# Pre-norm transformer block on one core: normalised tokens split in place and turned by DMA transposes

## The reference

```python
x = x + attn(layernorm(x), W_qk, W_v, slope)
x = x + ffn(layernorm(x), w_gate, w_up, w_down)

def attn(x, W_qk, W_v, slope):          # causal, one head of 128
    scores = (x @ W_qk) @ x.T / sqrt(128) + (kpos - qpos) * slope
    return softmax(where(qpos >= kpos, scores, -inf)) @ (x @ W_v.T)

def ffn(x, w_gate, w_up, w_down):       # int32 weights times 1/127, hidden width 384
    return (silu(x @ w_gate.T) * (x @ w_up.T)) @ w_down.T
```

## Time and profile before

| what | us |
|---|---|
| median of 3 runs (144.57 to 145.28) | 144.62 |
| the profiled execution, its own time | 145.67 |
| its span, first to last instruction | 143.9 |
| PE, DVE, ACT, POOL busy in the span | 122.8, 120.7, 110.7, 97.6 |

### The profile page before, as it was taken

How to read it: one execution, slowest core, us unless ns; L and a number is a source line. 1 busy time by engine, 2 the same in 40 slices (tenths; PEclk the granted TensorE clock), 3 DMA queues, 4 the chain that set the end, 5 groups by cost and what they waited for, 6 DMA issues and landing times.

```text
span 143.9 us, 3450 instructions
## 1 busy us (share of the span) xinstructions
PE 122.8 (85%) x1215; PEld 91.9 (64%) x1215; DVE 120.7 (84%) x341; ACT 110.7 (77%) x251; POOL 97.6 (68%) x157
## 2 busy tenths in 40 slices
PE   0239658999999999999999998979998899999942
PEld 0028345867987769978779776657755656675541
DVE  0729989998697996969996969999879999988781
ACT  4034588999976999949999769985699978999830
POOL 6490769964993454992438943798999999646810
PEclk9999999999999999999999999999999999999995
DMA  4997000000000000000000000000000222022204
GB/s 129 221 244 190 0 0 2 7 2 0 5 0 0 5 0 2 5 0 0 0 5 0 5 0 2 2 5 0 5 0 0 77 77 66 12 73 77 77 0 146
DMA packets 9811, 5.18 MB, mean 36 GB/s; under 512 B 448, under 2 KB 9792, under 8 KB 9792
## 3 DMA queue, kind: packets, MB, share of 16 engines
q1 hardware_dynamic: 9792, 4.92, 12.2%
HBM read 2.82 MB, written 2.10 MB: 34 GB/s over the span
## 4 chain that ended last, share of the span: by engine, by line
PE 50%; DVE 23%; ACT 9%; POOL 7%; DMA 4%; issue 3%; SPq 2%; DVEq 0%
PE work_ps L556 7%; POOL hidden_lo L411 6%; PE attn_ps L571 5%; PE attn_ps L573 4%; PE attn_ps L572 4%; PE score_ps L504 4%; PE score_ps L506 4%; DVE probsT_lo L824 4%; PE score_ps L505 4%; DMA wd_int<-in_L_ffn_w_down_dram 4%; DVE biased L841 3%; PE score_ps L595 2%; PE score_ps L592 2%; DVE stats L726 2%; ACT silu L1069 2%
## 5 line engine op out<-in xcount | busy, mean ns | idle before, releaser
L571 PE MATMUL attn_ps<-v_hi,probsT_hi 128*128 128x128 f16 x144 | 25.8, 219 | 3.0 <-DVE xs L851 2.4
L824 DVE TENSOR_TENSOR probsT_lo<-work_ps,probsT_hi 128x512 f16<-128x512 f32 (+3 forms) x48 | 25.2, 552 | 3.5 <-ACT probsT_hi L1007 3.4
L1007 ACT CAST probsT_hi<-work_ps 128x512 f16<-128x512 f32 (+3 forms) x48 | 21.4, 484 | 7.7 <-PE work_ps L556 7.4
L992 ACT ACTIVATE probs<-biased,neg_max 128x128 f32<-128x128 f32 (+7 forms) x32 | 25.0, 783 | 1.9 <-DVE neg_max L841 1.9
L841 DVE CUSTOM_DVE_ANT_0 biased<-score_ps,bias,neg_score_scale 128x128 f32<-128x128 f32 (+7 forms) x32 | 25.8, 806 | 0.6 <-PE score_ps L506 0.6
L573 PE MATMUL attn_ps<-v_hi,probsT_lo 128*128 128x128 f16 x144 | 25.8, 219 | 0.0
L572 PE MATMUL attn_ps<-v_lo,probsT_hi 128*128 128x128 f16 x144 | 25.8, 219 | 0.0
L556 PE MATMUL work_ps<-ident,probs 128*128 128x128 f32 x144 | 21.4, 274 | 0.2 <-DVE probsT_lo L824 0.2
L411 POOL TENSOR_TENSOR hidden_lo<-hidden,hidden_hi 128x512 f16<-128x512 f32 x13 | 17.6, 1375 | 5.1 <-ACT hidden_hi L1075 5.1
L556 PEld LDWEIGHTS work_ps<-ident,probs 128*128 128x128 f32 x144 | 16.5, 141 | 3.2 <-DVE probsT_lo L824 0.5
L437 POOL TENSOR_TENSOR xT_lo<-whole,xT_hi 128x512 f16<-128x512 f32 x8 | 9.3, 1163 | 13.6 <-ACT whole L986 13.6
(11 more groups left out here) (135 smaller groups left out, 346.7 us busy)
## 6 DMA issues: line engine op xcount, KB each, us to landing
out_dram<-xs SPq DMA_DIRECT2D x7, 256.0 KB, 2.7
xs<-in_L_attn_x_dram SPq DMA_DIRECT2D x3, 512.0 KB, 7.4
xs<-in_L_attn_x_dram SPq DMA_DIRECT2D x2, 256.0 KB, 3.0
out_dram<-xs SPq DMA_DIRECT2D x2, 128.0 KB, 1.9
wgu_int<-in_L_ffn_w_gate_dram SPq DMA_DIRECT2D x1, 192.0 KB, 3.1
wgu_int<-in_L_ffn_w_up_dram SPq DMA_DIRECT2D x1, 192.0 KB, 3.4
wd_int<-in_L_ffn_w_down_dram SPq DMA_DIRECT2D x1, 192.0 KB, 5.1
wqk_in<-in_L_attn_W_qk_dram SPq DMA_DIRECT2D x1, 64.0 KB, 2.9
```

Source lines behind the costliest of these rows:

```text
L571: pe.matmul(attn_ps[:, 0:D], p_hi, v_j, start=(j == 0), stop=False)
L824: dve.tensor_tensor(probsT_lo[:, i % 2, cols], work_ps[:, bank, 0:n], probsT_hi[:, i % 2, cols], ALU.subtract).then_inc(work_emptied, 1)
L992: act.activation(probs[:, i % 2, 0:n], biased[:, i % 2, 0:n], ACT.Exp, bias=neg_max[:, i:i + 1], scale=-1.0, accum_out=prob_sum[:, i:i + 1 ...
L1007: act.copy(probsT_hi[:, i % 2, CW * h:CW * h + n], work_ps[:, bank, 0:n]).then_inc(probsT_hi_ready, 1)
```

## The change

Normalisations 0 and 1 stay as they were. For 2 and 3 (LN1 of batches 2 and 3) and 4 to 7 (all LN2), PE transposes nothing: ACT casts `xn` in `SBUF` to `xn_hi` (`token_high`), POOL subtracts into `xn_lo` (`token_low`), and SP issues one DMA transpose for each part and half (`turn`; 24 in all, 128 KB each, ahead of all stores in SP's queue). `x2T_hi` and `x2T_lo` get room for all eight chunks. The copies of x to `whole` and the lo parts from it go, for q they stay. DVE's `split_x2` goes. `down` alternates between two PSUM banks.

Statistics move: DVE takes those of 2 in round 0, steps 0 to 3; those of b+3 in rounds 0 to 2, steps 4 to 7; of 6 in the last round, steps 0 to 3; of 7 as before. So LN2 of batches 0 and 1 is normalised in rounds 2 and 3, and each POOL job of a round has its place by a written order. `token_high` stands in ACT's stream at the places of `tokens_at`: normalisation 2 in round 0, step 7, and round 1, step 0; normalisation b+2 in round b, steps 5 and 6 (b = 1, 2, 3); 6 behind the silus of chunks 0 and 1; 7 behind those of chunks 3 and 4.

Core of the diff (the rest replaces run-time indices, no longer needed, and renames the counts of the banks):

```diff
+    BY_DMA = 2
+    NROUND = 2 * B
+    def parts_at(b, i):
+        if b == B - 1 or i == 0:
+            return []
+        return [part for part in prologue[i - 1:i] if part[0] != "xT" or b + 1 < BY_DMA]
...
-        x2T_hi, x2T_lo = (part[:, B % 2, :].rearrange("p (c n) -> p c n", c=2) for part in (xT_hi, xT_lo))
+        x2T_hi = sb("x2T_hi", [P, NCH, CW], F16)
+        x2T_lo = sb("x2T_lo", [P, NCH, CW], F16)
+        xn_hi = sb("xn_hi", [P, 2, TB, D], F16)
+        xn_lo = sb("xn_lo", [P, 2, TB, D], F16)
...
-        x2T_ps = work_ps[:, 2, :]
...
-        down_ps = attn_ps[:, :]
+        down_ps = [attn_ps[:, :], work_ps[:, 2, :]]
...
+            def turn(n, h):
+                par, tiles = n % 2, slice(CT * h, CT * (h + 1))
+                cols = slice(CW * h, CW * (h + 1))
+                if n < B:
+                    sp.wait_ge(scores_ready, TB * (n - 1))
+                for part, ready, o in ((xn_hi, xn_hi_ready, xT_hi if n < B else x2T_hi),
+                                       (xn_lo, xn_lo_ready, xT_lo if n < B else x2T_lo)):
+                    o = o[:, par, cols] if n < B else o[:, HALVES * (n - B) + h, :]
+                    sp.wait_ge(ready, split_before(n, h) + 1)
+                    sp.dma_start_transpose(o.rearrange("p (t q) -> p t q", q=P),
+                                           part[:, par, tiles, :].rearrange("p t d -> p (t d)"))\
+                      .then_inc(xT_landed[par][h], 16)
+            for n in range(BY_DMA, NROUND):
+                for h in range(HALVES):
+                    turn(n, h)
...
-                if isinstance(n, int) and n > B + 1:
-                    pool.wait_ge(x2T_filled, HALVES * (n - B - 1))
-                elif not (isinstance(n, int) and n == 0):
-                    pool.wait_ge(work_filled, place(n - 2, ("xT", HALVES - 1))[1] + 1)
+                if n > BY_DMA:
+                    pool.wait_ge(xn_lo_ready, split_before(n, 0))
+                elif n:
+                    pool.wait_ge(work_filled, filled(("xT", n - 1, HALVES - 1)))
...
+            def token_low(n, h):
+                tiles = slice(CT * h, CT * (h + 1))
+                pool.wait_ge(xn_hi_ready, split_before(n, h) + 1)
+                pool.tensor_tensor(xn_lo[:, n % 2, tiles, :], xn[:, tiles, :], xn_hi[:, n % 2, tiles, :], ALU.subtract)\
+                    .then_inc(xn_lo_ready, 1)
...
-            for b in range(B - 1):
-                nxt = (b + 1) % 2
-                for part in prologue:
-                    if by_pool(part):
-                        split_low(b + 1, nxt, *part)
+            for kind, h in prologue[:2 * HALVES]:
+                split_low(1, 1, kind, h)
+            norm(2)
+            for h in range(HALVES):
+                token_low(2, h)
+            for b in range(1, B - 1):
                 norm(b + 2)
-            for part in prologue[:HALVES]:
-                split_low(B, B % 2, *part)
-            norm(B + 1)
-            moments(B + 2)
-            centre(B + 2)
+                for h in range(HALVES):
+                    split_low(b + 1, (b + 1) % 2, "q", h)
+                for h in range(HALVES):
+                    token_low(b + 2, h)
+            for n in (B + 1, B + 2):
+                norm(n)
+                for h in range(HALVES):
+                    token_low(n, h)
             moments(B + 3)
-            scale(B + 2)
             hidden_low(1, 1)
             centre(B + 3)
             hidden_low(2, 0)
             scale(B + 3)
             hidden_low(3, 1)
-            for m in range(2, NCH // 2 - 1):
-                for par in range(2):
-                    hidden_low(2 * m + par, par)
-            for par in range(2):
-                hidden_low(NCH - 2 + par, par)
+            for h in range(HALVES):
+                token_low(B + 3, h)
+                hidden_low(4 + h, h)
+            for c in range(6, NCH):
+                hidden_low(c, c % 2)
...
+                elif b < BY_DMA:
+                    taken(("xT", b, h))
                 else:
-                    taken(b - 1, ("xT", h))
...
-                    if not (isinstance(c, int) and c < 2):
-                        pe.wait_ge(x2T_ready, c - 1)
+                    n, h = B + c // HALVES, c % HALVES
+                    pe.wait_ge(xT_landed[n % 2][h], landed(n))
...
-            def transpose_x2(c, par):
-                pe.wait_ge(xn_ready, HALVES * B + c)
-                if not (isinstance(c, int) and c == 2):
-                    pe.wait_ge(x2T_ready, c - 2)
-                for j in range(CT):
-                    m = pe.transpose(x2T_ps[:, P * j:P * (j + 1)], xn[:, CT * par + j, :], ident[:, :])
-                m.then_inc(x2T_filled, 1)
...
-                    elif not (isinstance(c, int) and c == NCH - 1):
-                        pe.wait_ge(result_ready, c)
+                    elif 1 < c < NCH - 1:
+                        pe.wait_ge(result_ready, c - 1)
...
-                    if not final:
-                        transpose_x2(c + par + 2, par)
                     if not (first and par == 0):
-                        down(c + par - 1, 1 - par)
+                        down(c + par - 1, 1 - par, down_ps[1 - par])
...
+                if j == 0 and B <= n < B + 3:
+                    dve.wait_ge(attn_added, TB * (n - B + 1))
...
-                    if final and i % (TB // 2) < HALVES:
-                        for j in range(CT):
-                            statistics(b + 2 + i // (TB // 2), CT * (i % (TB // 2)) + j)
...
-                    if not final and i < TB // 2:
-                        statistics(b + 2, 2 * i)
-                        statistics(b + 2, 2 * i + 1)
+                    early, late = i < TB // 2, i >= TB // 2
+                    for n in [2] * (b == 0 and early) + [b + 3] * (not final and late) + [B + 2] * (final and early):
+                        statistics(n, 2 * (i % (TB // 2)))
+                        statistics(n, 2 * (i % (TB // 2)) + 1)
...
-            def split_x2(c, par):
-                dve.wait_ge(x2T_hi_ready, c - 1)
-                dve.tensor_tensor(x2T_lo[:, par, :], x2T_ps, x2T_hi[:, par, :], ALU.subtract).then_inc(x2T_ready, 1)
...
+            def token_high(n, h):
+                tiles = slice(CT * h, CT * (h + 1))
+                act.wait_ge(xn_ready, HALVES * n + h)
+                if n >= BY_DMA + 2:
+                    act.wait_ge(xT_landed[n % 2][h], landed(n - 2))
+                act.copy(xn_hi[:, n % 2, tiles, :], xn[:, tiles, :]).then_inc(xn_hi_ready, 1)
+            def tokens_at(b, i):
+                if (b, i) in ((0, TB - 1), (1, 0)):
+                    return [(2, b)]
+                return [(b + 2, i - 5)] if b and i in (5, 6) else []
...
-            def copy_x2_high(c, par):
-                act.wait_ge(x2T_filled, c - 1)
-                act.copy(x2T_hi[:, par, :], x2T_ps).then_inc(x2T_hi_ready, 1)
...
-                    if not final:
-                        copy_x2_high(c + par + 2, par)
+                    for n, h in {0: [(B + 2, 0)], 1: [(B + 2, 1)], 3: [(B + 3, 0)], 4: [(B + 3, 1)]}.get(c + par, []):
+                        token_high(n, h)
```

More of the change, by code:

```diff
@@ L105, in at, with by_pool, emptied, copied_high @@
+    def by_pool(key):
+        return key[0] in ("xT", "q") and key[1] > 0
+    def emptied(key):
+        return sum(by_pool(k) == by_pool(key) for k in ring[:ring_index[key] + 1])
+    def copied_high(key):
+        return sum(k[0] != "P" for k in ring[:ring_index[key] + 1])
+    VECTOR_TAKES = sum(not by_pool(k) for k in ring)
     def at(buffer, half, columns):
-        if isinstance(half, int):
-            return buffer[:, half, columns]
-        return buffer[:, ds(half, 1), columns].rearrange("p a n -> p (a n)")
+        return buffer[:, half, columns]
@@ L538, in scores @@
                 if i in (0, 2):
-                    taken(b - 1, ("q", i // 2))
-                if not (isinstance(t, int) and t < 2):
+                    taken(("q", b, i // 2))
+                if t >= 2:
                     pe.wait_ge(biased_ready, t - 1)
```

168 lines of the change are left out of this document (69 added, 99 removed).

## The result

| | before | after |
|---|---|---|
| median of the runs | 144.59 us (4 runs, 144.50 to 145.28) | 151.81 us (4 runs, 151.02 to 152.72) |
| ratio | | 1.049, 95% interval 1.045 to 1.053 |
| profiled execution / its span | 145.67 / 143.9 us | 152.27 / 150.4 us |
| PE, DVE, ACT, POOL busy in 104.6 to 142 | 33.11, 33.27, 29.97, 27.41 | 28.67, 27.25, 26.52, 31.59 |

The change makes the kernel 4.9% slower; 151.4 us had been forecast.

What follows compares the result with a forecast made beforehand. PE was taken to bound the middle rounds, an ACT-POOL-PE loop the FFN. FFN lateness 5.3 (containing +0.8 and -1.4) and clock 1.5 on 143.9 gave span 150.7, median 151.4 us; range 146.8 to 157.0.

Steps and rivals of the forecast that it cites:

- What bounds the kernel: PE sets the middle rounds; the FFN is a loop over ACT's `hidden_hi`, POOL's `hidden_lo` and PE's `down`.
- Rounds 0 to 2, +0.8: Rounds 0 to 2: statistics 3 x 0.48, PE's transposes gone 2 x -0.73, PE's wait for POOL's q split 0.85 us.
- The turning, 3 us and hidden: DMA transposes in round 1 and FFN: 3 us each, covered by 4.6 and about 4.1 us, cost 0.
- rival 1: DMA transposes in round 1 and chunk 6 are slow, 5 to 7.4 us each: 156.6 us, past 160 without overlap; chance 0.15.
- Last round, -1.4, FFN 0.6 sooner: Last round: fewer DVE statistics and PE transposes bring weights of tiles 6 and 7 1.4 us earlier; FFN begins 0.6 earlier.
- ACT's wait, 3.3 us: FFN start: ACT stands still 3.3 us for `xn` of normalisation 6, with `hidden_hi` and silus queued behind.
- POOL's list: FFN: work ahead of `hidden_lo` makes chunk 1's end at 119.6, chunk 3's silu 6.1 us late, chunk 7's 5.3 late.
- Clock, +1.5: FFN start: PE idles before `down(0)` and `down(1)`, its clock falls to half, costing 1.5 us; bounds 0 and 4.
- From the span to the median: Whole run: span 150.7 us plus 1.77 gives 152.5 profiled; the median lies 1.05 lower, 151.4 us.
- Rival 2: FFN: ACT's wait counts but POOL's late `hidden_lo` is caught up, about 3 us less, 147 to 148 us; chance 0.13.
- rivals 3 and 4: Whole kernel: faster through relief of PE, DVE and ACT, 140.7 us, chance 0.10; or no change, near 144.6, chance 0.04.
- Rival 3: FFN start: 140.7 us if normalisation 6's `xn` is ready by 104.5 and 7's small instructions before chunk 1's `hidden_hi`; chance 0.10.

Runs made afterwards that it cites:

- the run without it: Changed kernel with early casts of normalisation 5, plus POOL splitting half 0 of q before it scales in rounds 1 and 2; 148.10 us, ratio 1.023.
- the run with both edits: Changed kernel with normalisation 5's last-round casts two steps earlier and normalisation 7's small instructions ahead of normalisation 6's second lo part; 147.11 us, ratio 1.015.

## Why the prediction was right, step by step

The forecast was 151.4 us and the result 151.81; the mechanism of the main term, POOL's and ACT's lists at the start of the FFN, is as told. That the sum comes out to 0.4 us is in part luck: several terms were off and cancel.

- **What bounds the kernel.** Right. The FFN is set by ACT, POOL and PE in a ring. Of the changed kernel's chain of waits between 104 and 124, POOL's `hidden_lo` is 24.8% and POOL's normalisations and lo parts some 41%, though PE is the engine with most busy time over the whole span (81%).
- **Rounds 0 to 2, +0.8.** The sum is near, its parts are wrong. From the values of tile 0 to those of tile 7, round 0 took 19.12 us against 18.07, so it lost 1.05 where 0.48 had been counted; 0.67 of it lies between tiles 5 and 6, where DVE waited 1.5 us for POOL to have read the buffer of statistics, which I had not seen. Rounds 1 and 2, from tile 7 to tile 7, each took 19.86 against 20.02: -0.16 twice, where +0.60 (0.48 - 0.73 + 0.85) and -0.25 had been counted. The step that failed in round 1 is the +0.85 for `qT_lo`. PE did wait, 0.53 us, but round 1 came out as short as round 2, which has no such wait, and as short as in the run without it: it was slack. Together +0.73. The tile 7 of round 2 nevertheless stands at 82.46 against 82.14, only 0.32 later, because this execution was 0.41 us ahead before round 0 began (23.62 against 24.03); why is open.
- **The turning, 3 us and hidden.** Landing took 2.5 us in the median (2.4 to 4.2). "Advanced Engine Details and Errata", X-Bar Transpose (TRN2), in the Trainium skill, says as fast as plain DMAs; the trace agrees within 0.6 us (the plain 128 KB took 1.9 us). The estimate of 5.2 us from "VectorE: DVE Perf Modes" in the Trainium skill does not fit: four blocks land in 2.5 us, so rival 1 falls. Its mechanism is real all the same: with the number of turns doubled it costs 5 us. The term lacked SP's own 1.2 us for each turn.
- **Last round, -1.4, FFN 0.6 sooner.** The size is wrong, the start is right by luck. From the values of tile 7 of round 2 to the third silu of chunk 0 it took 21.43 us against 22.48: -1.05. That silu begins at 103.89 against 104.62, 0.7 sooner, because of the 0.41 above.
- **ACT's wait, 3.3 us.** 3.16, released by POOL's `xn`. `xn` is wanted at 104.6 and there at 107.7, as walked. In the run with early casts the wait is gone and 3.3 us return.
- **POOL's list.** The second cast was to end at 112.1 (112.2), `hidden_lo` of chunk 1 at 119.6 (119.5), chunk 3's silu at 122.0 (121.97), chunk 7's at 139.3 (139.91). All durations came from rows of the kernel before. Up to the third chunk two of them were off and cancel: the ten small instructions took 3.9 us, not 3.55, and the pair of `hidden_lo` 2.27, not 2.73. At chunk 7 it was 0.6 us short: `hidden_lo` of chunk 5 ended at 137.4, not 137.1, and from there to the silu it took 2.5 us, not 2.2.
- **Clock, +1.5.** The step that failed, though the sum hides it. The clock did fall to half, between 108 and 110, as PE had been idle since 106.5 or so before `down(0)`. But it was full again by 116, and PE waited only 1.88 us before `down(1)`, where 3 to 6 had been forecast, so `down(1)` ran at full clock and the half clock lay beside ACT's and POOL's late chain. The run with PE kept busy shows that the clock before `down(0)` was not on the path; it also shows that the price was well reckoned, 2.05 us against 2.2, once the fall does lie before `down(1)`. In the place of the 1.5 us stand the 0.6 at chunk 7 and 0.6 in the tail: from chunk 7's first silu to the end of the span 10.5 us against 9.9. The chain there goes through DVE's `hidden_lo` of chunk 6, which took 1.67 us where 0.7 was meant, with `hidden` of chunk 7 behind it.
- **From the span to the median.** The last step took the profiled execution to be 1.05 us above the median, as in the kernel before; here it was 0.46 above. That is the other way than the span, which was 150.4 against 150.7.
- **Rivals.** Rival 2 (half of it) did not come, rivals 3 and 4 neither: for them normalisation 6 had to start by 98, and it started near 101. That start alone is not enough: with the casts earlier it was 95.5, and that kernel is 2.6% slower. Rival 3 had a second condition, the small instructions of 7 done before `hidden_hi` of chunk 1, and it was not met there (113.5 against 108.2) nor in the run with both edits (111.2 against 108.8). With chunks 4 to 7 undone it was nearly met (107.8 against 107.6), and the time is that of the kernel before or up to 0.6% less.

## What to carry to other kernels

Work taken off the busiest engine gained nothing here, where the stage is a ring of three engines; in such a stage walk the list of each engine in order and look at what newly stands ahead of the instruction that the ring waits for. A step that is given a new producer (here a cast on ACT) puts a wait into that engine's list too, and what is queued behind it, here `hidden_hi`, is late as well. Where a change has several parts, keep those whose wait has cover: here the turns of attention could stay at no loss, and giving up those late in the FFN, with all that hung on them, won 4 us. And before an edit is priced by a difference of times, compare the granted clock in the stretch that decides in both kernels: an edit can win time on one engine and give part of it back because PE then stands longer.
